# Involution weights loaded behind the first expert layer and prepared in the second norm

## The chip, the cores and the metric

One Trainium2 chip, one core of it. The time is the device time of one execution in microseconds (us), the median of several runs. TensorE multiplies matrices, VectorE and ScalarE work on elements, GpSimd does elements and issues scattered transfers, SyncE issues the other transfers. The profile names their rows PE (PEld for its weight loads), DVE, ACT, POOL and SP; a q behind the name is the engine's instruction queue.

## The reference, cut to what matters

Four layers, each a mixer and a mixture of experts, run over x of shape (8, 32, 32, 128). Before each of the two the rows are normalised over the channels, and the result is added to x. The change touches the mixer of the second layer, an involution: each pixel has its own 3 x 3 kernel for each of 8 groups of 16 channels, computed from the pixel itself by two small matrices.

```python
def _ln_c(v, eps=1e-06):
    m = jnp.mean(v, axis=-1, keepdims=True)
    s = jnp.var(v, axis=-1, keepdims=True)
    return (v - m) / jnp.sqrt(s + eps)

def _L1_conv_ref(x, W1, b1, W2, b2):       # W1 (128, 32), W2 (32, 72)
    ...
    wgt = jnp.einsum('bhwc,cd->bhwd', x, W1) + b1
    wgt = jnp.einsum('bhwd,de->bhwe', wgt, W2) + b2
    wgt = wgt.transpose(0, 3, 1, 2).reshape(b, G, 1, kk, h, w)
    ...
    patches = jnp.stack([xp[:, i:i + h, j:j + w, :] for i in range(K) for j in range(K)], axis=3)
    ...
    out = jnp.einsum('bgokhw,bgckhw->bgchw', wgt, out)
    ...

x = x + _L0_conv_ref(_ln_c(x), ...)
t = t + _L0_ffn_ref(_ln_t(t), ...)
x = x + _L1_conv_ref(_ln_c(x), L1_conv_W1, L1_conv_b1, L1_conv_W2, L1_conv_b2)
t = t + _L1_ffn_ref(_ln_t(t), ...)
...
```

## The kernel before, in words

The kernel is a row of blocks: constants, then for each layer a norm (`norm_mixer`) and a mixer with its expert layer (`mixer_fractal`, `mixer_involution`, and so on), at the end `finish`. In a block each engine has its own list of instructions, written out by hand, and runs it in order; semaphores order the engines among each other. A block ends when all its engines are through. The residual rows stay on the chip in `k.x`, 64 tiles of 128 rows by 128 channels, 8 tiles to an image.

**The expert layers.** The router of a mixer sends each row to a place in memory that belongs to its expert (`dispatched`), and GpSimd issues these scattered writes. `Experts.sync` lets SyncE load the sorted rows back tile by tile through a ring of 16 buffers (line 993); TensorE, ScalarE, VectorE work on a tile, and GpSimd scatters the result to `returned` (line 1245). SyncE is 16 tiles ahead, so it has issued its last load well before the block ends. `Experts` takes a function `load_next`, which SyncE calls behind its last tile; the involution's expert layer already loads the weights of the third layer's mixer that way (`SplineWeights.load`), the first expert layer loads nothing.

**The norm blocks.** SyncE loads the returned rows of the eight images, one transfer each (line 277). With two choices per row GpSimd adds the two (line 285); the first layer has one choice, and GpSimd has nothing to do in the second norm. VectorE adds each image to the residual (line 302) and takes statistics of its 8 tiles (line 304). After the last image it finishes the statistics (lines 240 to 246), ScalarE takes the root (line 349), and VectorE and ScalarE normalise the tiles between them (lines 321 and 356). TensorE turns each image to channel-major order (line 341) and ScalarE copies it into `channel_major` with its border (line 364). The third norm already has a preparation in front of the image loop: `spline.prepare` on VectorE, `spline.turn` on TensorE.

**The involution's block.** It opens with a preparation. SyncE loads ten small pieces: W2 and b1 four times each, for four groups of 32 partitions (lines 1710 and 1711), W1 and b2 (lines 1712 and 1713), and waits for them; then come the bias columns, the gate (lines 506 and 507) and the expert weights (line 513). GpSimd makes the gather matrices with a memset and two selects (lines 1726 to 1731). VectorE, once the ten loads are there, copies W1 four times side by side (line 1828), splits W2 in three bf16 parts (lines 1831 to 1835), places these (line 1839) and spreads them over the channels with 24 copies (line 1843), the last 8 of them for the row of the bias. TensorE then turns the bias row into 9 columns (line 1740) and VectorE copies these to `b2` (line 1848). Behind that the first product of the block runs (line 1751, `hidden(0, 0)`), which needs W1 and the image alone; ScalarE and VectorE split its result in bf16 parts (lines 1797 to 1803, 1857 to 1865), and the loop over 8 images of 2 x 9 taps begins: TensorE computes the kernel entries (lines 1761 and 1762), VectorE multiplies them with the shifted image (line 1877), TensorE adds up (line 1770). The router of an image runs between the taps of the next image.

Of the kernel before, what the change touches and what calls it, by code (L numbers as in the profile page):

```python
# [245 lines left out]
    ch.link(dve.scalar_tensor_tensor(out=var4, in0=spare, scalar=4.0 / C, in1=var4, op0=ALU.mult, op1=ALU.add))  # L246


def norm_mixer(k, layer, spline=None):

    nc = k.nc
    choices = FFN[layer - 1]["K"] if layer else 0
# [12 lines left out]
    with ExitStack() as ctx, nc.Block() as block:  # L265
        if choices:
# [1003 lines left out]
        sp.dma_start(dst[:, j:j + 1], v.rearrange("(c a) -> c a", a=1)).then_inc(sem.h, 16)  # L1270


def mixer_fractal(k):

# [21 lines left out]
    with ExitStack() as ctx, nc.Block() as block:  # L1296
# [345 lines left out]
    route.done()  # L1642


def mixer_involution(k, load_next):

# [2 lines left out]


    nc, i = k.nc, k.ins
    RED = i["L1_conv_W1"].shape[1]
    TAPS = 9
    GROUPS = i["L1_conv_W2"].shape[1] // TAPS
    GC = C // GROUPS
    PER = 2 * TAPS
    names = ("inv_loaded", "inv_prep", "inv_bias", "inv_ones", "inv_hidden", "inv_part", "inv_rest", "inv_kernel", "inv_product",
             "inv_sum", "inv_stored")  # L1660
    s = {n: k.sem(n) for n in names}
    loads = 16 * (4 * 2 + 2)
    PREP = 1 + 5 + 8 + 3 + 1

    def when(name, n):
        return s[name].h, s[name].base + n
# [2 lines left out]
    with ExitStack() as ctx, nc.Block() as block:  # L1669
# [12 lines left out]
        used = 2 * FFN[1]["E"] * FFN[1]["F"]  # L1682
        spans = k.wts[:, used:used + TAPS * C].bitcast(BF16).rearrange("p (x n) -> p x n", x=2)
        span_a, span_b = spans[:, 0], spans[:, 1]
        gather = k.wts[:, used + TAPS * C:used + 2 * TAPS * C].rearrange("p (t c) -> p t c", t=TAPS)
        left = used + 2 * TAPS * C
# [3 lines left out]
        bias_row = k.flat(k.rows1)[0:1, 0:TAPS * C]  # L1690

        def mixed(b):

# [4 lines left out]
        w1 = sb("reduce_w", [P, RED])  # L1698
        w1r = sb("reduce_w_four_times", [P, 4, RED])
        w2 = sb("span_w", [P, GROUPS * TAPS])  # L1700
        w2p = sb("span_w_parts", [P, 5, GROUPS * TAPS], BF16)
        b2row = sb("span_b_row", [1, GROUPS * TAPS])
        b1 = sb("reduce_b", [P, 1])
        b2 = sb("span_b", [P, TAPS])

        @block.sync
        def _(sp):
            for g in range(4):
                rows = slice(RED * g, RED * (g + 1))
                sp.dma_start(w2[rows, :], i["L1_conv_W2"]).then_inc(s["inv_loaded"].h, 16)  # L1710
                sp.dma_start(b1[rows, :], i["L1_conv_b1"].rearrange("(c a) -> c a", a=1)).then_inc(s["inv_loaded"].h, 16)
            sp.dma_start(w1[:], i["L1_conv_W1"]).then_inc(s["inv_loaded"].h, 16)
            sp.dma_start(b2row[:], i["L1_conv_b2"].rearrange("(a c) -> a c", a=1)).then_inc(s["inv_loaded"].h, 16)
# [8 lines left out]

        @block.gpsimd
        def _(pool):

            pool.memset(gather, 1.0).then_inc(s["inv_ones"].h, 1)
            pool.wait_ge(*when("inv_ones", 1))
            pool.affine_select(out=gather, in_=gather, compare_op=ALU.is_ge, fill=0.0, base=0,
                               pattern=[[P, TAPS], [-TAPS, C]], channel_multiplier=1).then_inc(s["inv_ones"].h, 1)
            pool.wait_ge(*when("inv_ones", 2))  # L1730
            pool.affine_select(out=gather, in_=gather, compare_op=ALU.is_ge, fill=0.0, base=TAPS - 1,
                               pattern=[[-P, TAPS], [TAPS, C]], channel_multiplier=-1).then_inc(s["inv_ones"].h, 1)
            route.send_most(pool)
            ex.gpsimd(pool)

        @block.tensor
        def _(pe):
            pe.wait_ge(*when("inv_prep", PREP - 1))
            for tap in range(TAPS):
                ins = pe.matmul(k.ps[:, 0, tap:tap + 1], bias_row[:, tap * P:(tap + 1) * P], k.ident[0:1, 0:1],  # L1740
                                start=True, stop=True)
            ins.then_inc(s["inv_bias"].h, 1)
# [44 lines left out]

        @block.scalar
        def _(act):
            act.wait_ge(*when("inv_loaded", loads))  # L1790
# [33 lines left out]

        @block.vector
        def _(dve):
            dve.wait_ge(*when("inv_loaded", loads))
            dve.tensor_copy(w1r[:], w1[:].unsqueeze(1).to_broadcast([P, 4, RED])).then_inc(s["inv_prep"].h, 1)

            ch = Chain(dve, s["inv_prep"], s["inv_prep"].base + 1)  # L1830
            ch.link(dve.tensor_copy(w2p[:, 0, :], w2[:]))
            ch.link(dve.tensor_tensor(w2[:], w2[:], w2p[:, 0, :], ALU.subtract))
            ch.link(dve.tensor_copy(w2p[:, 1, :], w2[:]))
            ch.link(dve.tensor_tensor(w2[:], w2[:], w2p[:, 1, :], ALU.subtract))
            ch.link(dve.tensor_copy(w2p[:, 2, :], w2[:]))
            for x, parts in ((3, (0, 1, 0, 1)), (4, (2, 0, 2, 1))):
                for g, part in enumerate(parts):
                    rows = slice(RED * g, RED * (g + 1))
                    ch.note(dve.tensor_copy(w2p[rows, x, :], w2p[rows, part, :]))
            ch.settle()  # L1840
            for p, dst, src in ((P, span_a, w2p[:, 3, :]), (P, span_b, w2p[:, 4, :]), (1, bias_row, b2row[:])):
                for g in range(GROUPS):
                    ins = dve.tensor_copy(
                        dst[:, g * GC * TAPS:(g + 1) * GC * TAPS].rearrange("p (c t) -> p c t", t=TAPS),
                        src[:, g * TAPS:(g + 1) * TAPS].unsqueeze(1).to_broadcast([p, GC, TAPS]))
                ins.then_inc(s["inv_prep"].h, 1)
            dve.wait_ge(*when("inv_bias", 1))
            dve.tensor_copy(b2[:], k.ps[:, 0, 0:TAPS]).then_inc(s["inv_prep"].h, 1)
            dve.wait_ge(*when("inv_prep", PREP))

            def leave(b, half):

                h = 2 * b + half
# [489 lines left out]
def build(nc, ins, out):  # L2343
    with ExitStack() as ctx:
        k = Core(nc, ctx, ins, out)
        constants(k)
        norm_mixer(k, 0)
        mixer_fractal(k)
        norm_mixer(k, 1)
        with ExitStack() as spline_ctx:  # L2350
            weights = SplineWeights(k, spline_ctx)
            mixer_involution(k, weights.load)
            norm_mixer(k, 2, weights)
            mixer_spline(k, weights)
        norm_mixer(k, 3)
# [31 lines left out]
```

## Time and profile before

| what | us |
|---|---|
| median of 3 runs | 2304.84 (2304.82 to 2305.32) |
| profiled execution: its span, first to last instruction | 2301.3 |
| second norm's block, first transfer to the next block's first | 557.43 to 602.91 |
| involution's block, opening to its first product (line 1751) | 602.91 to 618.92 |
| TensorE busy over the span | 1745.5 (76%) |
| VectorE busy over the span | 1545.8 (67%) |
| mean granted clock of TensorE, of full speed | 0.880 |

The profiled execution has no other time than its span. A timeline row reads: start, duration, engine, line, operation, what it writes <- what it reads, shape, count, and in brackets how long the engine stood idle before it and what released it. Rows of several instructions give the time from the first to the last. In the rows of stretches each engine's busy time is followed by its count of instructions, and at the end stand the granted clock (1.00 is 2.4 GHz, 0.50 is 1.2 GHz), the share of the DMA engines and GB/s.

### The profile page before, as it was taken

The numbers are of one execution on the slowest core, as the hardware profiler recorded it, in microseconds if no ns is written. First come the engines' busy times: TensorE is split into PE (matmuls) and PEld (weight loads), VectorE is DVE, ScalarE is ACT, GpSimd is POOL, SyncE is SP. The second block draws the span as 40 slices with busy tenths as digits, with TensorE's granted clock in tenths as the row PEclk, the third lists the DMA queues.
The fourth block names the chain that finished last, engine by engine and source line by source line (L and its number), as shares of the span: only waits on it lengthen the run. The fifth ranks groups of instructions, "written<-read, shape, count | busy, mean of one in ns | idle before, by whom it ended". The sixth has DMA issues, their size and how long they took to land. (4 is left out here: it accounts for less than half of the span.)

```text
span 2301.3 us, 46320 instructions
## 1 busy us (share of the span) xinstructions
PE 1745.5 (76%) x10964; PEld 1375.2 (60%) x10981; DVE 1545.8 (67%) x4675; ACT 1183.7 (51%) x2659; POOL 981.1 (43%) x969
## 2 busy tenths in 40 slices
PE   1488666994488888999981776879639999888992
PEld 1133666994244343899981344767627777687992
DVE  6898887776677777654448676646486777754554
ACT  2445776894323333776663333556535444455661
POOL 0000134552004343664444177777630355466662
PEclk9799767997699999999995787789869999989996
DMA  3001102223201011232224112233332011123326
GB/s 75 1 1 37 47 28 59 69 75 89 75 3 35 24 33 54 66 97 67 60 57 145 45 53 78 71 99 101 99 137 88 22 36 38 50 72 98 92 76 223
DMA packets 183551, 153.81 MB, mean 67 GB/s; under 512 B 40290, under 2 KB 162818, under 8 KB 183358
## 3 DMA queue, kind: packets, MB, share of 16 engines
q1 hardware_dynamic: 153406, 92.37, 14.8%
q0 software_dynamic: 29952, 59.26, 7.6%
q8 instruction: 74, 1.21, 0.2%
q14 instruction: 119, 0.97, 0.1%
HBM read 85.33 MB, written 68.79 MB: 67 GB/s over the span
## 5 line engine op out<-in xcount | busy, mean ns | idle before, releaser
L1245 POOL DMA_INDIRECT returned<-rows_second_choice x488 | 482.3, 988 | 306.9 <-DVE rows_second_choice L1175 114.3
L1042 PE MATMUL psum<-rows_first_choice 128*128 128x128 f32 x3360 | 470.7, 281 | 7.8 <-DVE rows_first_choice L1156 7.8
L1052 PE MATMUL psum<-expert_weights,rows_first_choice 128*128 x2784 | 425.6, 289 | 57.6 <-ACT rows_first_choice L1109 18.4
L1042 PEld LDWEIGHTS psum<-rows_first_choice 128*128 128x128 f32 x3360 | 428.9, 198 | 9.8 <-DVE rows_first_choice L1156 9.6
L1052 PEld LDWEIGHTS psum<-expert_weights,rows_first_choice 128*128 128x128 f32 x2784 | 360.1, 196 | 95.4 <-issue 89.4
L1109 ACT ACTIVATE rows_first_choice<-psum,bias_columns 128x128 f32<-128x128 f32 x1104 | 323.5, 368 | 162.9 <-PE psum L1042 148.8
L820 POOL DMA_INDIRECT dispatched<-rows_first_choice,slot x192 | 194.9, 1015 | 492.4 <-DVE rows_second_choice L720 439.4
L820 POOL DMA_INDIRECT dispatched<-rows_second_choice,slot x192 | 187.7, 978 | 58.5 <-issue 58.2
L1150 DVE COPY rows_first_choice<-expert_weights 128x512 f32 (+1 forms) x272 | 107.1, 394 | 144.0 <-PE psum L1042 118.9
L341 PE MATMUL psum<-identity,rows_first_choice 128*128 128x128 f32 x256 | 45.9, 341 | 193.1 <-DVE rows_first_choice L321 143.4
L1175 DVE SCALAR_TENSOR_TENSOR rows_second_choice<-psum,rows_second_choice,rows_first_choice 128x128 f32<-128x128 f32 x344 | 119.3, 347 | 98.8 <-PE psum L1052 96.3
L820 POOL DMA_INDIRECT dispatched<-rows_first_choice,expert_weights x64 | 62.0, 968 | 266.8 <-DVE rows_first_choice L718 249.4
L1092 ACT ACTIVATE rows_first_choice<-expert_weights 128x512 f32 x216 | 136.8, 634 | 49.0 <-issue 48.8
L341 PEld LDWEIGHTS psum<-identity,rows_first_choice 128*128 128x128 f32 x256 | 38.1, 179 | 200.2 <-DVE rows_first_choice L321 180.0
L1156 DVE COPY rows_first_choice<-psum 128x128 f32<-128x128 f32 x488 | 137.4, 282 | 10.9 <-PE psum L1034 10.2
L1034 PE MATMUL psum<-identity,rows_second_choice 128*128 128x128 f32 x488 | 137.1, 282 | 6.4 <-DMA rows_second_choice<-dispatched 6.4
L1112 ACT ACTIVATE rows_first_choice<-rows_first_choice,rows_second_choice 128x128 f32 x344 | 141.2, 410 | 0.0
L1162 DVE TENSOR_TENSOR rows_first_choice<-rows_first_choice,psum 128x256 f32<-128x256 f32 x144 | 60.6, 421 | 111.9 <-ACT rows_first_choice L1102 101.1
L2287 PE MATMUL psum<-channel_major 128*128 128x512 f32 x256 | 131.7, 598 | 1.2 <-ACT channel_major L2205 1.2
L2221 ACT ACTIVATE att_work<-psum 128x512 f32<-128x512 f32 x128 | 73.1, 596 | 89.9 <-PE psum L2287 87.6
L2296 PEld LDWEIGHTS psum<-rows_second_choice,rows_first_choice 128*128 128x128 f32 x680 | 88.7, 191 | 47.0 <-issue 34.9
L2296 PE MATMUL psum<-rows_second_choice,rows_first_choice 128*128 128x128 f32 x680 | 90.3, 276 | 5.4 <-DVE rows_first_choice L2255 5.4
(372 smaller groups left out, 3272.8 us busy)
## 6 DMA issues: line engine op xcount, KB each, us to landing
rows_second_choice<-dispatched SPq DMA_DIRECT2D x488, 65.0 KB
expert_weights<-returned SPq DMA_DIRECT2D x12, 1024.0 KB, 10.4
rows_second_choice<-returned SPq DMA_DIRECT2D x8, 1024.0 KB, 10.7
returned<-rows_second_choice POOLq DMA_INDIRECT x488
expert_weights<-in_L_ffn_w SPq DMA_DIRECT2D x3, 2048.0 KB, 8.3
residual<-in_x SPq DMA_DIRECT2D x8, 512.0 KB, 7.2
rows_first_choice<-returned SPq DMA_DIRECT2D x4, 1024.0 KB, 8.8
out<-residual SPq DMA_DIRECT2D x8, 512.0 KB, 6.0
```

Source lines behind the costliest of these rows:

```text
L820: pool.indirect_dma_start(out=self.k.dispatched, out_offset=bass.IndirectOffsetOnAxis(ap=self.slot[:, b % 2, c, t:t + 1], axis=0), in_=sel ...
L1034: pe.transpose(k.ps[:, self.PSX + u % 2, 0:P], self.rt[:, u, 0:C], k.ident[:]).then_inc(self.s["x_turned"].h, 1)
L1042: ins = pe.matmul(k.ps[:, self.PSH + u % 2, j * P:(j + 1) * P], self.wc[:, u % 2, j * P:(j + 1) * P], self.xt[:, u % 2, :], start=True, st ...
L1052: ins = pe.matmul(self.result_bank(u), self.gs[:, u % self.HB, j * P:(j + 1) * P], self.second[:, bass.ds(e, 1), j, :].rearrange("p a c -> ...
L1092: act.activation(self.wc[:, u % 2, :], self.first[:, bass.ds(e, 1), :].rearrange("p a f -> p (a f)"), ACT.Copy).then_inc(self.s["w_copied" ...
L1109: ins = act.activation(self.hs[:, u % self.HB, cols], k.ps[:, self.PSH + u % 2, cols], f["act"], bias=self.bcol[:, bass.ds(e * self.J + j, ...
L1112: act.activation(self.wb[:, u % 4, :], self.b2rows[:, bass.ds(e, 1), :].rearrange("p a c -> p (a c)"), ACT.Copy, scale=self.rt[:, u, C + 1 ...
L1156: dve.tensor_copy(self.xt[:, u % 2, :], k.ps[:, self.PSX + u % 2, 0:P]).then_inc(self.s["x_copied"].h, 1)
L1175: ins = dve.scalar_tensor_tensor(out=self.ys[:, u, :], in0=self.result_bank(u), scalar=weight, in1=self.wb[:, u % 4, :], op0=ALU.mult, op1 ...
L1245: pool.indirect_dma_start(out=k.returned[0:N * self.K, :], out_offset=bass.IndirectOffsetOnAxis(ap=self.rt[:, u, C:C + 1].bitcast(I32), ax ...
L2287: pe.matmul(k.ps[:, g % 4, :], xft[:, b * IMG + j * P:b * IMG + (j + 1) * P], xft[:, b * IMG + h * BANK:b * IMG + (h + 1) * BANK], start=T ...
L2296: ins = pe.matmul(k.ps[:, 4 + h, t * P:(t + 1) * P], r2[g % 3][:, t * P:(t + 1) * P], val[:, b, j * P:(j + 1) * P], start=(j == 0 and t == ...
```

## The change

A class `InvolutionWeights` now holds the involution's weights and the code that prepares them. The ten loads are given to the first expert layer as its `load_next`, so that SyncE issues them behind the last tile of rows and waits for them there. In the second norm GpSimd makes the gather matrices, VectorE runs the preparation before the image loop (with the bias row spread first and the two spans behind it), TensorE turns the bias row before its transposes, into PSUM bank 4, and VectorE copies the 9 columns behind the statistics of the last image. The involution's block begins with its first product. Most of the preparation's buffers move from tiles of their own into parts of larger tiles that are free at that time.

```diff
-def norm_mixer(k, layer, spline=None):
+def norm_mixer(k, layer, spline=None, involution=None):
...
+        if involution:
+            @block.gpsimd
+            def _(pool):
+                involution.make_gather(pool)
+
...
             if spline:
                 spline.prepare(dve)
+            if involution:
+                involution.prepare(dve)
             for b in range(B):
...
                 for t in range(b * TPB, (b + 1) * TPB):
                     ch.note(dve.bn_stats(k.stats[:, t, :], k.x[:, t, :]))
+            if involution:
+                involution.take_bias(dve)
             ch = Chain(dve, s["norm_step"], s["norm_step"].base + B * per)
             ch.settle()
             finish_stats(dve, k, ch)
...
             if spline:
                 spline.turn(pe)
+            if involution:
+                involution.turn(pe)
...
-        ex = Experts(k, 0, ctx, route)
+        ex = Experts(k, 0, ctx, route, load_next)
...
+class InvolutionWeights:
...
+        spare, temporary, last = k.flat(k.rows0)[:, N:], k.flat(k.rows1)[:, 2 * IMG:], k.wts[:, 12288 - 2 * P:]
...
+    def load(self, sp):
+        i, RED, sem = self.k.ins, self.RED, self.s["inv_loaded"]
+        for g in range(4):
+            rows = slice(RED * g, RED * (g + 1))
+            sp.dma_start(self.w2[rows, :], i["L1_conv_W2"]).then_inc(sem.h, 16)
+            sp.dma_start(self.b1[rows, :], i["L1_conv_b1"].rearrange("(c a) -> c a", a=1)).then_inc(sem.h, 16)
+        sp.dma_start(self.w1[:], i["L1_conv_W1"]).then_inc(sem.h, 16)
+        sp.dma_start(self.b2row[:], i["L1_conv_b2"].rearrange("(a c) -> a c", a=1)).then_inc(sem.h, 16)
+        sp.wait_ge(*self.when("inv_loaded", self.loads))
+
+    def prepare(self, dve):
...
+        dve.wait_ge(*self.when("inv_loaded", self.loads))
+        dve.tensor_copy(self.w1r[:], self.w1[:].unsqueeze(1).to_broadcast([P, 4, RED])).then_inc(s["inv_prep"].h, 1)
...
+        for p, dst, src in ((1, self.bias_row, self.b2row[:]), (P, self.span_a, w2p[:, 3, :]), (P, self.span_b, w2p[:, 4, :])):
...
+    def take_bias(self, dve):
+        dve.wait_ge(*self.when("inv_bias", 1))
+        dve.tensor_copy(self.b2[:], self.k.ps[:, self.BANK, 0:self.TAPS]).then_inc(self.s["inv_prep"].h, 1)
+
+    def turn(self, pe):
+        pe.wait_ge(*self.when("inv_prep", self.PREP - 3))
+        for tap in range(self.TAPS):
+            ins = pe.matmul(self.k.ps[:, self.BANK, tap:tap + 1], self.bias_row[:, tap * P:(tap + 1) * P],
+                            self.k.ident[0:1, 0:1], start=True, stop=True)
+        ins.then_inc(self.s["inv_bias"].h, 1)
+
+    def make_gather(self, pool):
+        s, gather, TAPS = self.s, self.gather, self.TAPS
+        pool.memset(gather, 1.0).then_inc(s["inv_ones"].h, 1)
...
-def mixer_involution(k, load_next):
+def mixer_involution(k, weights, load_next):
...
         @block.sync
         def _(sp):
-            for g in range(4):
...
-            sp.wait_ge(*when("inv_loaded", loads))
             ex.sync_early(sp)
...
         def _(pe):
-            pe.wait_ge(*when("inv_prep", PREP - 1))
...
-            pe.wait_ge(*when("inv_ones", 3))
-            pe.wait_ge(*when("inv_prep", PREP))
-
...
-        mixer_fractal(k)
-        norm_mixer(k, 1)
+        involution = InvolutionWeights(k, ctx)
+        mixer_fractal(k, involution.load)
+        norm_mixer(k, 1, involution=involution)
...
-            mixer_involution(k, weights.load)
+            mixer_involution(k, involution, weights.load)
```

## Rows read from the trace of the kernel before

**Rows 1.** The page's chain that ended last, by engine.
```profile
SPq 1%; DMA 0%; DVE 0%; issue 0%; DVEq 0%
```

**Rows 2.** Busy time, involution opening: us, PE, PEld, DVE, ACT, POOL, clock, DMA, GB/s.
```profile
602.91:618.92 16.01, 3.99 (x19) 3.94 (x19) 5.76 (x39) 0.00 (x0) 3.48 (x3) 0.52 0.40 66
```

**Rows 3.** Timeline of the opening of the involution's block.
```profile
601.61 1.03 ACT L364 ACTIVATE channel_major<-psum 128x1024 f32<-128x1024 f32 x1 [0.28 <-PE psum L341]
602.91 1.06 POOL L1726 MEMSET expert_weights<- 128x1152 f32 x1 [54.22 <-POOLq L265]
602.91 0.36 SPq L1710 DMA_DIRECT2D span_w<-in_L_conv_W  x1
...
605.33 1.21 POOL L1731 TENSOR_SCALAR_AFFINE_SELECT expert_weights<-expert_weights 128x1152 f32<-128x1152 f32 x1
...
608.51 0.23 DVE L1828 COPY reduce_w_four_times<-reduce_w 128x128 f32<-128x128 f32 x1 [9.83 <-DMA span_b_row<-in_L_conv_b]
...
613.30 1.21 DVE L1843 COPY rows_second_choice<-span_b_row 1x144 f32<-1x144 f32 x8
614.21 1.46 SPq L513 DMA_DIRECT2D expert_weights<-in_L_ffn_W  x2
...
614.57 3.99 PE L1740 MATMUL psum<-identity,rows_second_choice 1*128 1x1 f32 x18 [13.00 <-DVE rows_second_choice L1843]
618.60 0.17 DVE L1848 COPY span_b<-psum 128x9 f32<-128x9 f32 x1 [4.08 <-PE psum L1740]
...
618.92 2.05 PE L1751 MATMUL psum<-channel_major,reduce_w_four_times 128*128 128x512 f32 x2 [0.35 <-DVE span_b L1848]
...
626.34 0.63 PE L1762 MATMUL psum<-rows_first_choice,expert_weights 128*128 128x512 bf16 x1 [5.37 <-DVE rows_first_choice L1865]
```

**Rows 4.** Timeline of the second norm's block.
```profile
557.43 6.82 SPq L277 DMA_DIRECT2D expert_weights<-returned  x6
...
561.28 1.23 DVE L302 TENSOR_TENSOR residual<-residual,expert_weights 128x1024 f32<-128x1024 f32 x1 [15.14 <-DMA expert_weights<-returned]
...
583.82 0.27 DVE L240 TENSOR_TENSOR mean<-bn_stats 128x64 f32<-128x64 f32 x1
```

**Rows 5.** Stretches around the opening, and the whole tap loop.
```profile
603.00:603.50 0.50, 0.00 (x0) 0.00 (x0) 0.00 (x0) 0.00 (x0) 0.50 (x1) 0.91 0.00 0
603.50:604.00 0.50, 0.00 (x0) 0.00 (x0) 0.00 (x0) 0.00 (x0) 0.47 (x1) 0.50 0.06 9
621.00:626.00 5.00, 0.00 (x0) 0.07 (x2) 2.17 (x5) 3.08 (x5) 0.00 (x0) 0.50 1.04 391
630.50:631.00 0.50, 0.50 (x3) 0.37 (x2) 0.00 (x0) 0.50 (x1) 0.00 (x0) 0.78 0.00 0
626.30:921.70 295.40, 249.63 (x913) 118.85 (x927) 218.27 (x604) 93.13 (x142) 101.54 (x104) 0.95 0.10 30
```

**Rows 6.** Timeline of TensorE, a later product of the same kind.
```profile
640.77 1.02 PE L1751 MATMUL psum<-channel_major,reduce_w_four_times 128*128 128x512 f32 x2
```

**Rows 7.** Timeline of the third norm's opening, GpSimd beside VectorE.
```profile
1206.72 11.43 SPq L277 DMA_DIRECT2D expert_weights<-returned  x6
...
1206.80 0.29 DVE L1944 MEMSET hats_at_zero<- 128x1 f32 x9 [5.32 <-PEq L1669]
...
1216.34 17.77 POOL L285 TENSOR_TENSOR expert_weights<-expert_weights 128x1024 f32<-128x1024 f32 x6 [13.60 <-issue]
...
1218.70 3.35 DVE L302 TENSOR_TENSOR residual<-residual,expert_weights 128x1024 f32<-128x1024 f32 x1 [4.46 <-POOL expert_weights L285]
...
1223.65 1.69 DVE L302 TENSOR_TENSOR residual<-residual,expert_weights 128x1024 f32<-128x1024 f32 x1
```

**Rows 8.** What SyncE's queue waited for: total, times, longest, in us.
```profile
SPq L1296 <- PEq L1296: 36.8, 1, 36.8
```

**Rows 9.** Timeline of TensorE, the first products of the gate.
```profile
670.82 1.85 PE L559 MATMUL psum<-gate_w,turned_rows 128*128 128x8 f32 x16
```

**Rows 10.** Line 1857: minimum, median, maximum in ns; first and last start.
```profile
L1857 DVE SCALAR_TENSOR_TENSOR hidden_rest<-psum,reduce_b,rows_first_choice x16: 742/751/752, 621.9 to 891.3; 128x512 f32<-128x512 f32 x16
```

More of the change, by code:

```diff
@@ L1270, in load_columns, with mixer_fractal @@
         sp.dma_start(dst[:, j:j + 1], v.rearrange("(c a) -> c a", a=1)).then_inc(sem.h, 16)
-def mixer_fractal(k):
+def mixer_fractal(k, load_next):
     nc, i = k.nc, k.ins
@@ L1642, in mixer_fractal, with __init__, sb, when @@
     route.done()
-def mixer_involution(k, load_next):
+class InvolutionWeights:
+    TAPS = 9
+    BANK = 4
+    PREP = 1 + 5 + 8 + 3 + 1
+    def __init__(self, k, ctx):
+        nc, i = k.nc, k.ins
+        self.k = k
+        self.RED = RED = i["L1_conv_W1"].shape[1]
+        self.GROUPS = i["L1_conv_W2"].shape[1] // self.TAPS
+        self.GC = C // self.GROUPS
+        self.loads = 16 * (4 * 2 + 2)
+        def sb(name, shape, dt=F32):
+            return ctx.enter_context(nc.sbuf_tensor(name, shape, dt))
+        TAPS, GROUPS = self.TAPS, self.GROUPS
+        self.used = used = 2 * FFN[1]["E"] * FFN[1]["F"]
+        spans = k.wts[:, used:used + TAPS * C].bitcast(BF16).rearrange("p (x n) -> p x n", x=2)
+        self.span_a, self.span_b = spans[:, 0], spans[:, 1]
+        self.gather = k.wts[:, used + TAPS * C:used + 2 * TAPS * C].rearrange("p (t c) -> p t c", t=TAPS)
+        spare, temporary, last = k.flat(k.rows0)[:, N:], k.flat(k.rows1)[:, 2 * IMG:], k.wts[:, 12288 - 2 * P:]
+        wide = GROUPS * TAPS
+        self.w1, self.w2 = spare[:, 0:RED], spare[:, RED:RED + wide]
+        self.w1r = last[:, 0:4 * RED].rearrange("p (a r) -> p a r", a=4)
+        self.b2row = last[0:1, P:P + wide]
+        self.bias_row = temporary[0:1, 0:TAPS * C]
+        self.w2p = temporary[:, TAPS * C:TAPS * C + 5 * wide // 2].bitcast(BF16).rearrange("p (x n) -> p x n", x=5)
+        self.b1 = sb("reduce_b", [P, 1])
+        self.b2 = sb("span_b", [P, TAPS])
+        self.s = {n: k.sem(n) for n in ("inv_loaded", "inv_prep", "inv_bias", "inv_ones")}
+    def when(self, name, n):
+        return self.s[name].h, self.s[name].base + n
+    def load(self, sp):
[8 more added lines that the diff above has]
+    def prepare(self, dve):
+        s, w2, w2p, RED, TAPS, GROUPS, GC = self.s, self.w2, self.w2p, self.RED, self.TAPS, self.GROUPS, self.GC
+        dve.wait_ge(*self.when("inv_loaded", self.loads))
+        dve.tensor_copy(self.w1r[:], self.w1[:].unsqueeze(1).to_broadcast([P, 4, RED])).then_inc(s["inv_prep"].h, 1)
+        ch = Chain(dve, s["inv_prep"], s["inv_prep"].base + 1)
+        ch.link(dve.tensor_copy(w2p[:, 0, :], w2[:]))
+        ch.link(dve.tensor_tensor(w2[:], w2[:], w2p[:, 0, :], ALU.subtract))
+        ch.link(dve.tensor_copy(w2p[:, 1, :], w2[:]))
+        ch.link(dve.tensor_tensor(w2[:], w2[:], w2p[:, 1, :], ALU.subtract))
+        ch.link(dve.tensor_copy(w2p[:, 2, :], w2[:]))
+        for x, parts in ((3, (0, 1, 0, 1)), (4, (2, 0, 2, 1))):
+            for g, part in enumerate(parts):
+                rows = slice(RED * g, RED * (g + 1))
+                ch.note(dve.tensor_copy(w2p[rows, x, :], w2p[rows, part, :]))
+        ch.settle()
+        for p, dst, src in ((1, self.bias_row, self.b2row[:]), (P, self.span_a, w2p[:, 3, :]), (P, self.span_b, w2p[:, 4, :])):
+            for g in range(GROUPS):
+                ins = dve.tensor_copy(
+                    dst[:, g * GC * TAPS:(g + 1) * GC * TAPS].rearrange("p (c t) -> p c t", t=TAPS),
+                    src[:, g * TAPS:(g + 1) * TAPS].unsqueeze(1).to_broadcast([p, GC, TAPS]))
+            ins.then_inc(s["inv_prep"].h, 1)
+    def take_bias(self, dve):
[10 more added lines that the diff above has]
+        pool.memset(gather, 1.0).then_inc(s["inv_ones"].h, 1)
+        pool.wait_ge(*self.when("inv_ones", 1))
+        pool.affine_select(out=gather, in_=gather, compare_op=ALU.is_ge, fill=0.0, base=0,
+                           pattern=[[P, TAPS], [-TAPS, C]], channel_multiplier=1).then_inc(s["inv_ones"].h, 1)
+        pool.wait_ge(*self.when("inv_ones", 2))
+        pool.affine_select(out=gather, in_=gather, compare_op=ALU.is_ge, fill=0.0, base=TAPS - 1,
+                           pattern=[[-P, TAPS], [TAPS, C]], channel_multiplier=-1).then_inc(s["inv_ones"].h, 1)
@@ L1653, in mixer_involution @@
+def mixer_involution(k, weights, load_next):
     nc, i = k.nc, k.ins
[L1654 to L1657, printed above, removed]
+    RED, TAPS, GROUPS, GC = weights.RED, weights.TAPS, weights.GROUPS, weights.GC
+    w1r, b1, b2, span_a, span_b, gather = (weights.w1r, weights.b1, weights.b2, weights.span_a, weights.span_b,
+                                           weights.gather)
     PER = 2 * TAPS
-    names = ("inv_loaded", "inv_prep", "inv_bias", "inv_ones", "inv_hidden", "inv_part", "inv_rest", "inv_kernel", "inv_product",
-             "inv_sum", "inv_stored")
+    names = ("inv_hidden", "inv_part", "inv_rest", "inv_kernel", "inv_product", "inv_sum", "inv_stored")
@@ L1661, in mixer_involution @@
     s = {n: k.sem(n) for n in names}
-    loads = 16 * (4 * 2 + 2)
-    PREP = 1 + 5 + 8 + 3 + 1
     def when(name, n):
@@ L1681, in mixer_involution @@
         prods = [k.flat(k.rows1)[:, tail][:, 0:BANK], k.flat(k.rows1)[:, tail][:, BANK:2 * BANK]]
[L1682 to L1686, printed above, removed]
+        left = weights.used + 2 * TAPS * C
         mixed_first = k.wts[:, left:left + IMG]
@@ L1697, in mixer_involution @@
         ex = Experts(k, 1, ctx, route, load_next)
[L1698 to L1704, printed above, removed]
         @block.sync
         def _(sp):
-            for g in range(4):
[L1709 to L1713, printed above, removed]
-            sp.wait_ge(*when("inv_loaded", loads))
             ex.sync_early(sp)
@@ L1724, in _ @@
         def _(pool):
[L1726 to L1732, printed above, removed]
             route.send_most(pool)
@@ L1737, in _ @@
         def _(pe):
-            pe.wait_ge(*when("inv_prep", PREP - 1))
[L1739 to L1742, printed above, removed]
-            pe.wait_ge(*when("inv_ones", 3))
-            pe.wait_ge(*when("inv_prep", PREP))
             LAG = 3
@@ L1789, in _ @@
         def _(act):
-            act.wait_ge(*when("inv_loaded", loads))
             def bias(b, half):
@@ L1826, in _ @@
         def _(dve):
[L1827 to L1849, printed above, removed]
             def leave(b, half):
```

1 line of the change is left out of this document (removed).

## The prediction

> **What bounds the kernel now.** I read the page's chain of waits first: it holds only the last 1.2% of the span, the output stage [rows 1]. The kernel is a row of blocks, and an engine enters the next block only when all have left the last, so the stage's own views decide. The busy times of the opening of the involution's block come second [rows 2]: in its first 16.01 us TensorE is busy 3.99 us, ScalarE not at all, VectorE 5.76 us. The reader is to see a block in which nothing but preparation runs. The timeline says in which order [rows 3]. SyncE issues ten small loads from 602.91 on; VectorE starts at 608.51, released by the last of them after 9.83 us idle; its preparation ends at 613.30 + 1.21 = 614.51; TensorE's bias products run from 614.57 to 618.56; VectorE copies them (0.17 us); the first useful product of the block (L1751) starts at 618.92. GpSimd's three operations (602.91 to 605.33 + 1.21 = 606.54) wait for nobody and nobody waits for them last. Then the timeline of the norm block before it, where the work goes [rows 4]: SyncE enters at 557.43, VectorE waits until 561.28 for the first returned rows and from there works without a gap until 583.82. The norm block is bound by VectorE, with 3.8 us of slack at its opening and none behind.
>
> **The change part by part.** All terms are differences in one profiled execution of 2301.3 us; its only time shown is that span, and the timed runs are 3.5 us longer, which I take as fixed.
>
> *The opening goes.* TensorE's first product needs only the channel-major image and the prepared weights, both there when the block opens. GpSimd and SyncE issue at 602.91; I put TensorE 0.04 us behind, at 602.95: 618.92 - 602.95 = 15.97 us less. The next thing late is the chain behind that product (ScalarE's split and VectorE's rest, up to TensorE's 626.34), which moves along unchanged.
>
> *The first product is quicker.* Today it runs with TensorE long cold: 2.05 us for the pair [rows 3]. The granted clock is still high after the norm's last transposes: 0.91 of full speed averaged over 603.0 to 603.5, and 0.50, the 1.2 GHz level, only from 603.5 on [rows 5]. A product that starts at 602.95 meets the 2.4 GHz level, at which the same pair takes 1.02 us later in the loop [rows 6]: 1.03 us less, bounds 0 and 1.03. TensorE then idles about 5.37 us as today [rows 3]. The level fell at 603.5, some 1.9 us after the last transposes, which ScalarE's last copy (601.61) had waited for; so it should be low again when the taps come, as it is now: from 626.34 until about 630.6, where the clock is 0.78 in a half microsecond [rows 5]. If the high level should last, these 4.3 us of work would take half, 2.1 us less. I take nothing for it.
>
> *VectorE's preparation enters the norm.* The same 38 instructions, 608.51 to 614.51, are 6.00 us, in another order (bias row first) at the same cost. In the third norm block, which already opens with such a preparation, VectorE starts 0.08 us behind SyncE [rows 7]; so here at 557.51, and it ends at 563.51 instead of being ready for the rows at 561.28: 2.23 us more, all of it on the path, since VectorE has no gap behind. 3.77 of the 6.00 us lie in the old wait. Were that cover gone, the price would be 6.0.
>
> *GpSimd now works beside VectorE.* Its three operations take 3.63 us alone and start together with the preparation. Before, they had VectorE to themselves, so the trace has no row of this pair. The nearest rows are in the third norm, where GpSimd adds while VectorE adds: the same 128x1024 addition took 1.23 us with GpSimd idle [rows 4], 1.69 beside it, and 3.35 once, at the start of the overlap [rows 7]. From below: 0, the preparation's copies being short and of one input, save two. From above: VectorE stands still for all of it, 3.63 us. I take the steady row, as a share: 3.63 x (1 - 1.23/1.69) = 1.0 us more.
> The Trainium skill speaks against this part: "SBUF — State Buffer", section "SBUF: two separate sides", says that the port pair which VectorE and GpSimd share is locked by whichever instruction comes first for its whole length, while the other waits. The row of 3.35 us looks like such a lock, the 1.69 us rows do not stand still so long.
>
> *The copy of the bias.* One VectorE copy of 0.17 us stands between the statistics and their finish: 0.17 more, bounds 0 and 0.3. Behind its wait are queued VectorE's finish of the statistics and, through it, ScalarE's root. The wait itself costs nothing: the bias products start when 22 of the 38 instructions are done, last 3.99 us [rows 3], and so end near 567, while the statistics run to 583.82 today. TensorE's transposes, queued behind those products, are not due before the statistics either.
>
> *The ten loads move* to SyncE's queue behind the last rows of the first expert layer. They take 608.51 - 602.91 = 5.6 us with their landing. SyncE today waits 36.8 us at the end of that block [rows 8], so they are hidden six times over; uncovered they would cost those 5.6 us. Nothing is queued behind them. In the involution's block SyncE goes straight to the bias columns, the gate and the expert weights. The gate's loads are over when the weights are issued, at 614.21 today [rows 3]; after the change that is 614.21 - 608.51 = 5.7 us into the block. Their first user is TensorE at 670.82 [rows 9], 67.9 us into the block today and 51 after the change. The weights now land while the first taps run instead of before them. VectorE's 16 instructions of line 1857, the first of which ran while the DMA engines moved 391 GB/s [rows 5], took 742 to 752 ns each [rows 10], so I charge nothing.
>
> *Sum:* -15.97 - 1.03 + 2.23 + 1.0 + 0.17 = -13.6 us. The span becomes 2287.7 and the median 2304.84 - 13.6 = 2291.2 us, 0.59% less. Every later block starts when the involution ends, so the gain should last to the end.
>
> **The rivals.**
> *Full lock:* VectorE gets nothing done during GpSimd's 3.63 us. Instead of 1.0 the term is 3.63: -11.0, 2293.9 us. For it, the 3.35 us row; against it, the 1.69 us rows, and that the preparation is mostly tiny copies. By the skill's rule of the lock, named above, this is the case that should come, at least for the two additions and whichever copies use both ports.
> *Clock kept:* the high level lasts until the taps: 2.1 us less again, 2289.1 us. For it, that TensorE comes to this gap at the high level, not the low one; against it, that it lasted some 1.9 us in the gap of today, and the gap before the taps is 5.4 us.
> *Gain hidden:* the loop's start, or the first router, turns out to be held by something that the preparation covered, such as the weights now landing amid the taps, or the loads are not hidden. Then the wait only changes its name: about 2303 us. Against it stand rows 8 to 10.
> *Slower:* TensorE's clock in the tap loop. The loop is TensorE's (busy 249.63 of 295.40 us) and its granted clock averages 0.95 [rows 5], that is 10% of it, 29.5 us, at the lower level. A loop that starts in another state could fall more often at the gaps between images. Each us at the low level does half its work, so it costs 0.5 us. The 13.6 us are eaten from 27.2 more such us on (19% of the loop), and it is slower by 0.2% from 36.4 on (22%). At 25% the time is 2304.84 - 13.6 + 22.2 = 2313.4 us. Against it: the falls come where the router's work opens gaps in TensorE, which does not change.
>
> **How the numbers follow.** Forecast 0.64, full lock 0.14, clock kept 0.10, gain hidden 0.07, slower 0.05. The likeliest case by itself reaches from 2289.1 to 2293.9. For the range I add the loss of the quick first product (1.0), the smallest contention (-1.0) and the clock's changes further on, of about 2 us: 2289.1 - 3.0 = 2286.1 to 2293.9 + 3.0 = 2296.9. About 0.2%, 4.6 us, is what a measurement of this kernel tells from no change. Faster by more: the first three cases and part of the fourth, 0.91; within: 0.05; slower: 0.04.
>
> **What would show it.** The norm block's first residual addition (L302) should start near 564.5 instead of 561.28, the block should end some 3.4 us later, near 606, and the first L1751 pair should follow the last norm copy within 0.5 us and take about 1 us. GpSimd's memset and two selects should lie beside VectorE's copies; if these stretch from 6 to over 9 us, the lock is right. The loads should be done near 526, far ahead of the block's end at 557. The interval from the first L1751 to the first expert tile should keep its length; if it grows by several us, look at the clock. The prediction is wrong if the first L1751 is released by a wait for anything but the block's opening, or if the tap loop grows by more than the opening saves.

## The result and the profile after

The changed kernel takes 2278.30 us (median of 4 runs, 2276.42 to 2279.92) against 2304.83 (4 runs, 2304.63 to 2305.32): ratio 0.9882 [0.9869, 0.9896], 26.5 us less. The forecast of 2291.2 us has the right sign and half the size; 2278.30 lies below its range.

The span is 2274.7 us, 26.6 less than before, and the mean granted clock 0.883 (before 0.880). I read the timeline at five places, in order of time. The first is the opening of the second norm, to be read beside [rows 4] and the preparation of [rows 3].

```profile
557.65 1.06 POOL L1742 MEMSET expert_weights<- 128x1152 f32 x1 [8.73 <-POOLq L1307]
557.65 6.90 SPq L277 DMA_DIRECT2D expert_weights<-returned  x6
557.68 1.10 DVE L1709 COPY expert_weights<-rows_first_choice 128x128 f32<-128x128 f32 x1 [11.31 <-PEq L1307]
557.83 0.99 DVE L1712 CAST rows_second_choice<-rows_first_choice 128x72 bf16<-128x72 f32 x1
558.78 1.22 POOL L1744 TENSOR_SCALAR_AFFINE_SELECT expert_weights<-expert_weights 128x1152 f32<-128x1152 f32 x1
558.86 1.22 DVE L1713 TENSOR_TENSOR rows_first_choice<-rows_first_choice,rows_second_choice 128x72 f32<-128x72 f32 x1
560.06 1.21 POOL L1747 TENSOR_SCALAR_AFFINE_SELECT expert_weights<-expert_weights 128x1152 f32<-128x1152 f32 x1
560.11 1.21 DVE L1714 CAST rows_second_choice<-rows_first_choice 128x72 bf16<-128x72 f32 x1
561.35 0.23 DVE L1715 TENSOR_TENSOR rows_first_choice<-rows_first_choice,rows_second_choice 128x72 f32<-128x72 f32 x1
...
564.66 1.85 DVE L1724 COPY expert_weights<-rows_second_choice 128x144 bf16<-128x144 bf16 x16
...
566.43 1.20 DVE L309 TENSOR_TENSOR residual<-residual,expert_weights 128x1024 f32<-128x1024 f32 x1
...
588.83 0.15 DVE L1731 COPY span_b<-psum 128x9 f32<-128x9 f32 x1
588.94 0.27 DVE L240 TENSOR_TENSOR mean<-bn_stats 128x64 f32<-128x64 f32 x1
```

The block opens at 557.65. Four of VectorE's small operations take 0.99 to 1.22 us, and each ends within 0.11 us behind GpSimd's operation beside it (GpSimd's end at 558.71, 560.00 and 561.27); once GpSimd is through, the same kind takes 0.23. The preparation lasts from 557.68 to 566.51, 8.83 us instead of 6.00. The first residual addition starts 8.78 us after the opening (before: 3.85).

The second and third places are the opening of the involution's block and the end of its tap loop, beside [rows 3].

```profile
607.78 0.37 SPq L993 DMA_DIRECT2D bias_columns<-in_L_ffn_b  x1
...
607.82 1.10 PE L1818 MATMUL psum<-channel_major,expert_weights 128*128 128x512 f32 x2 [1.37 <-PEq L265]
...
613.75 0.61 PE L1828 MATMUL psum<-rows_first_choice,expert_weights 128*128 128x512 bf16 x1 [4.83 <-DVE rows_first_choice L1906]
...
900.58 0.42 DVE L1161 COPY rows_first_choice<-expert_weights 128x512 f32 x1
```

```profile
913.21 0.41 DVE L1150 COPY rows_first_choice<-expert_weights 128x512 f32 x1
```

The first product comes 0.04 us behind the opening, released by it, and is a quick one. The taps start at 613.75, 12.59 us earlier than 626.34. At the expert layer's first copy of weights (the row behind is the kernel before's) 12.63 us are gained: the tap loop is what it was.

The fourth place is the opening of the third norm, before at 1206.72 [rows 7]:

```profile
1181.28 1.02 SPq L277 DMA_DIRECT2D expert_weights<-returned  x2
```

The gain is 25.44 us here, so another 12.8 us came in the second expert layer, which the change doesn't touch. From here to the end of the span it grows by 1.2 more. The fifth place is therefore the loop of that layer. First ScalarE's timeline in the kernel before, then what it waited for at this line (total, times, longest, in us), before and after.

```profile
1079.33 1.14 ACT L1109 ACTIVATE rows_first_choice<-psum,bias_columns 128x128 f32<-128x128 f32 x4 [0.46 <-PE psum L1042]
1080.34 0.42 ACT L1112 ACTIVATE rows_first_choice<-rows_first_choice,rows_second_choice 128x128 f32 x1
1086.14 1.14 ACT L1109 ACTIVATE rows_first_choice<-psum,bias_columns 128x128 f32<-128x128 f32 x4 [5.38 <-issue]
...
1122.73 1.14 ACT L1109 ACTIVATE rows_first_choice<-psum,bias_columns 128x128 f32<-128x128 f32 x4 [5.40 <-issue]
```

```profile
ACT rows_first_choice L1109 <- issue: 11.8, 7, 5.4
```

```profile
ACT rows_first_choice L1120 <- issue: 3.5, 12, 0.5
```

Twice ScalarE stood still for 5.4 us and waited for nothing that the profile shows, 36.6 us apart: where its loop over 16 tiles jumps back. After the change no such wait is over 0.5 us. What TensorE lost by it is in the stretches, before and after (us, PE, PEld, DVE, ACT, POOL, clock, DMA, GB/s):

```profile
1080.00:1090.00 10.00, 5.65 (x43) 5.42 (x42) 2.69 (x9) 3.53 (x13) 2.27 (x3) 0.91 0.18 50
1090.00:1100.00 10.00, 10.00 (x85) 10.00 (x85) 4.79 (x15) 6.90 (x25) 4.91 (x5) 0.92 0.16 46
1117.00:1127.00 10.00, 5.63 (x38) 5.40 (x38) 2.26 (x7) 3.10 (x12) 2.10 (x3) 0.76 0.18 50
```

```profile
1067.00:1077.00 10.00, 10.00 (x92) 10.00 (x91) 5.63 (x17) 7.66 (x28) 5.62 (x6) 1.00 0.27 73
```

TensorE idles 4.35 and 4.37 us and then works at a granted clock of 0.50, the 1.2 GHz level, for about 3.4 us behind the first stall and 5.0 behind the second. At half speed these cost 1.7 and 2.5 us; with the idle time that is an estimate of 12.9 us, as much as the 12.8 gained here. After the change TensorE is busy throughout, at 1.00. The DMA queues of the stretch 1080.5 to 1086.5 before, and of 1067 to 1073 after (the same jump back), say what happened (packets, MB, share of 16 engines):

```profile
q1 hardware_dynamic: 525, 0.25, 18.5%
q0 software_dynamic: 96, 0.20, 9.2%
q14 instruction: 4, 0.03, 1.7%
```

```profile
q1 hardware_dynamic: 576, 0.27, 19.5%
q0 software_dynamic: 97, 0.20, 9.8%
```

The stalled stretch holds four fetches of instructions, of 8 KB each, the other none. The same queue over the whole span, from the pages of before and after:

```profile
q14 instruction: 119, 0.97, 0.1%
```

```profile
q14 instruction: 109, 0.89, 0.1%
```

Of the twelve profiles behind this document the three with stalls show 119 such packets, the other nine 109 or 110. In ScalarE's program the change makes one difference ahead of this loop: the wait for the ten loads (`inv_loaded`) is gone, one instruction, and everything behind it stands one place earlier.

### The profile page after: what moved, and what is told of

Its sections match the earlier page's. It is cut to its first block and busy times, and to the rows that moved or that the text cites. A ratio compares the mean times of both kernels' runs of the same rounds, so it can differ in the third digit from the quotient of the medians.

```text
span 2274.7 us, 46334 instructions
## 1 busy us (share of the span) xinstructions
PE 1743.1 (77%) x10980; PEld 1372.8 (60%) x10981; DVE 1546.3 (68%) x4675; ACT 1182.3 (52%) x2659; POOL 978.9 (43%) x969
## 5 line engine op out<-in xcount | busy, mean ns | idle before, releaser
L1063 PE MATMUL psum<-expert_weights,rows_first_choice 128*128 x2784 | 423.1, 288 | 47.7 <-issue 13.5
## 6 DMA issues: line engine op xcount, KB each, us to landing
expert_weights<-returned SPq DMA_DIRECT2D x12, 1024.0 KB, 10.3
```

The source lines that it names most:

```text
L1063: ins = pe.matmul(self.result_bank(u), self.gs[:, u % self.HB, j * P:(j + 1) * P], self.second[:, bass.ds(e, 1), j, :].rearrange("p a c -> ...
```

## The experiments

My theory A: half of the gain has nothing to do with the preparation; it is the place of ScalarE's loop in its program. Its rival: the changed weights, or the earlier start, make the second expert layer run better. For the norm block: GpSimd's operations hold VectorE's small ones for their whole length (the lock), or only slow them.

**Only the wait removed** (the kernel before, without it)

```diff
-            act.wait_ge(*when("inv_loaded", loads))
```

> The kernel before, with one thing out: ScalarE's own wait for the ten loads at the head of the involution's block. It is covered by the wait behind it, so no work moves. Theory A (ScalarE's program: two stalls of 5.4 us of ScalarE in the second expert layer, at 1080.7 and 1117.3, come from how its loop lies in the program; one instruction less shifts it): the stalls go, and with them what the clock loses behind them, about 13 us in all, so about 2292 us, ratio near 0.994. Theory B (the stalls come from when the loop runs, beside which transfers; the changed kernel runs it 12.6 us earlier): nothing changes, 2304.8 us within 1.

2290.6 us, ratio 0.9937 [0.9921, 0.9954]. The third norm opens 12.9 us earlier (timeline), 11.8 of it gained behind the first tap, which starts 1.1 earlier; and the stalls are gone (waits of ScalarE's line):

```profile
ACT rows_first_choice L1109 <- issue: 3.7, 12, 0.5
```

```profile
1193.83 1.13 SPq L277 DMA_DIRECT2D expert_weights<-returned  x2
```

One instruction that never made ScalarE late is worth 13.5 us by the medians (2304.14 in these runs).

**The change with the wait put back**

```diff
+            act.wait_ge(*weights.when("inv_loaded", weights.loads))
```

> The changed kernel with the same wait of ScalarE put back at the head of the involution's block, where it is long fulfilled. Theory A: the two stalls of about 5.4 us come back in the second expert layer, and the time is about 2278.3 + 13 = 2291 us, ratio near 0.994, which is what the prediction's terms gave. Theory B: no stalls, 2278 us, ratio near 0.988.

2293.87 us, ratio 0.9953 [0.9936, 0.9969]: the change at the old place of the loop gains 10.3 us, which lies within the forecast's range. The stalls are back, both of them, and the third norm opens 15.6 us later than in the changed kernel; why the same two stalls cost more here than before the change is open.

```profile
1075.41 1.14 ACT L1120 ACTIVATE rows_first_choice<-psum,bias_columns 128x128 f32<-128x128 f32 x4 [5.62 <-issue]
...
1112.66 1.14 ACT L1120 ACTIVATE rows_first_choice<-psum,bias_columns 128x128 f32<-128x128 f32 x4 [5.53 <-issue]
...
1196.87 2.45 SPq L277 DMA_DIRECT2D expert_weights<-returned  x3
```

**GpSimd's three operations later** (the changed kernel; they wait for the norm's sixth image, away from the preparation)

```diff
+                pool.wait_ge(*when("norm_most", B - 2))
                 involution.make_gather(pool)
```

> The changed kernel with GpSimd's gather matrices made later: GpSimd waits for the sixth image's normalised tiles, when VectorE has a few us to spare, instead of starting beside VectorE's preparation. Theory lock (VectorE's first copies of 0.2 us took 1.0 to 1.2 us each because GpSimd's memset and selects held them): the preparation takes 6.0 us again instead of 8.8, the first residual addition starts 2.8 us earlier, and the time falls by 2.8 to about 2275.5 us. Rival (VectorE was slow at the block's opening for another reason, its code or the landing transfers): the copies stay at 1.0 to 1.2 us and the time stays at 2278 us.

2278.01 us, ratio 0.9878 [0.9861, 0.9895], no gain. But the preparation is back at 6.0 us, and the first addition comes 5.99 us after the opening instead of 8.78. Part of what was won is lost at the block's other end, where GpSimd now meets the normalisation:

```profile
559.10 0.23 DVE L1710 COPY expert_weights<-rows_first_choice 128x128 f32<-128x128 f32 x1 [11.32 <-PEq L1308]
559.24 0.19 DVE L1713 CAST rows_second_choice<-rows_first_choice 128x72 bf16<-128x72 f32 x1
...
565.05 1.20 DVE L310 TENSOR_TENSOR residual<-residual,expert_weights 128x1024 f32<-128x1024 f32 x1
...
601.83 1.21 POOL L1748 TENSOR_SCALAR_AFFINE_SELECT expert_weights<-expert_weights 128x1152 f32<-128x1152 f32 x1
603.68 1.09 PE L353 MATMUL psum<-identity,rows_first_choice 128*128 128x128 f32 x8 [1.96 <-DVE rows_first_choice L331]
```

The 48 normalisations of VectorE take 15.1 us in the block, 12.4 in the changed kernel; TensorE waits for them. The block takes 48.58 us, 1.55 less than the changed kernel's 50.13, but in this profile it opened 1.4 us later. TensorE's granted clock is 0.91 there from 420 to 440, in the first expert layer, where it is 1.00 in the changed kernel: about 1.7 us of TensorE's work, an estimate. What lowered it is open.

**The preparation out of the norm as well** (behind VectorE's last tile of the first expert layer; GpSimd as in the last one)

```diff
+            prepare_next(dve)          # in mixer_fractal, behind ex.vector(dve)
...
-            if involution:             # in norm_mixer
-                involution.prepare(dve)
```

> As the last one, and VectorE's 38 instructions of preparation moved once more, to the end of the first expert layer's block, where VectorE stands idle for 11 us (its temporaries lie 2176 columns further on, clear of the ring of rows). If the whole delay of the second norm's first residual addition is the preparation in front of it, that addition starts 3.8 us after the block opens, as before the change, instead of 8.8 us, and the time is about 2278.3 - 4.9 = 2273.4 us. Rival (the delay is partly the returned rows landing later): less than 2.8 us of it comes back, 2275.5 us or more.

2278.12 us, ratio 0.9881 [0.9865, 0.9898]. The preparation ran where VectorE was idle, from 548.04 to 554.37, and the first addition now waits for its rows (4.29 us after the opening). GpSimd again stretched the normalisation to 15.1 us. The block took 47.79 us (559.43 to 607.22) after 50.13 in the changed kernel, but opened 1.8 us later, behind the same 0.91 from 420 to 440, and the time did not move. These two runs left the place for GpSimd open: the norm block's opening, where VectorE now waits anyway.

**Preparation in the expert layer, GpSimd at the norm's opening**: the last kernel without the wait for `norm_most`, and with it, in the same runs, **the changed kernel once more**.

> The changed kernel with VectorE's preparation behind its last tile of the first expert layer (as in the run before it with that move) and GpSimd's three gather operations at the opening of the norm block, where VectorE now only waits for the first returned rows. No operation of GpSimd then lies beside one of VectorE. Lock theory: the first addition of the norm block starts about 4.3 us after the block's opening instead of 8.8, no normalisation is stretched at the end, the involution's block opens 4.5 us earlier against the norm block's opening, about 2274 us. Rival (the norm block is held by something else by then, the first returned rows or TensorE): as the two runs before, about 2278 us.

> The changed kernel itself, for its spread and as the mark for the three beside it: 2276 to 2280 us, no stall of ScalarE in the second expert layer.

2272.38 us (2271.75 to 2274.60), ratio 0.9866 [0.9850, 0.9882], against 2277.78 (2277.06 to 2279.50), ratio 0.9889 [0.9872, 0.9905]. The intervals overlap a little, but all runs of this version lie below all of the changed kernel's. Its norm block, in the timeline:

```profile
556.81 1.06 POOL L1741 MEMSET expert_weights<- 128x1152 f32 x1 [8.73 <-POOLq L1305]
556.82 7.14 SPq L277 DMA_DIRECT2D expert_weights<-returned  x6
...
559.23 1.21 POOL L1746 TENSOR_SCALAR_AFFINE_SELECT expert_weights<-expert_weights 128x1152 f32<-128x1152 f32 x1
561.32 1.22 DVE L307 TENSOR_TENSOR residual<-residual,expert_weights 128x1024 f32<-128x1024 f32 x1 [9.56 <-DMA expert_weights<-returned]
...
603.05 1.52 PE L1817 MATMUL psum<-channel_major,expert_weights 128*128 128x512 f32 x2 [1.38 <-PEq L265]
```

The block takes 46.2 us (50.1 in the changed kernel), 3.9 less where 4.5 was expected, and the normalisation is back at 12.4. The other 1.5 us between the medians are not located. So GpSimd delays VectorE's copies and its normalisations, and here its place was free where VectorE had nothing to do.

Not everything of VectorE is held. In the kernel before, GpSimd's additions of the third norm [rows 7] lie beside the statistics of most images, and those take as long as they do alone, at the end:

```profile
1225.37 1.64 DVE L304 BATCH_NORM_STATS2 bn_stats<-residual 128x6 f32<-128x128 f32 x8
...
1244.60 1.65 DVE L304 BATCH_NORM_STATS2 bn_stats<-residual 128x6 f32<-128x128 f32 x8
```

Beside the second norm's own 64 such instructions GpSimd's three operations were not tried.

**Where the loop stalls: two, three, four and five places on.** The changed kernel with the wait written 3, 5, 7 or 9 times; two such waits are put into one instruction, so these count 2, 3, 4 and 5 (ScalarE's rows in the trace: 7396, 7397, 7398 and 7399, against 7394 in the changed kernel and 7395 with one wait).

```diff
+            for _ in range(3):         # 5, 7, 9
+                act.wait_ge(*weights.when("inv_loaded", weights.loads))
```

> The changed kernel with ScalarE's wait for the ten loads written three times at the head of its list in the involution's block. Two of the three become instructions of their own, so ScalarE's loops of the second expert layer stand two instructions further on than in the changed kernel, one further than in the kernel before. Counted in ScalarE's program the second loop (258 instructions) begins at 2376 in the changed kernel (no stall), at 2377 in the kernel before (two stalls of 5.4 us) and at 2378 here. Theory A (a single bad place: the loop is just longer than one block of fetched instructions, and only where its first instruction is the last of a block does it touch a third): the stalls are gone again, third norm near 1181, about 2278 us. Rival B (from a certain place on the loop no longer fits): both stalls stay, third norm near 1197, about 2294 us.

> The changed kernel with the same wait written nine times, which puts ScalarE's two loops of the second expert layer five instructions further on: the first loop from 2116 to 2121, the second from 2376 to 2381. The bad place of theory A, 2377, repeats every 256 instructions, so 2121 is one too. Theory A: no stall at the second loop, but two of about 5.4 us at the first loop's two jumps back, near 977 and 1007 us, so again about 2294 us. Rival B (from a certain place on): the two stalls stay at the second loop, near 1070 and 1107. Rival C (the stalls hang on the time at which the loop is entered, not on its place): none or others, about 2278 us.

> The same with the wait written five times: loops three instructions further on (second loop from 2379). Theory A with 259: no stall, about 2278 us. Rival (bad places in no order that the count explains): stalls, at the first loop or the second, about 2294 us.

> The changed kernel with ScalarE's wait written seven times: loops four instructions further on than in the changed kernel (second loop from 2380 by the program's count). At five places on theory A, in the form that the bad place repeats every 256 instructions, failed: no stall at the first loop. In the trace 259 instructions, not 260, lie from one loop's jump back to the next loop's (the jump between the loops, which only falls through, leaves no record). If that jump is not there, the first loop's bad place is one earlier. Theory A with 259: two stalls of about 5.4 us at the first loop, near 977 and 1007 us, about 2294 us. If there is no stall, the repeat is not shown, and the one bad place stands alone.

| places on | us | stalls of 5 us and more |
|---|---|---|
| 0 (changed kernel) | 2277.78 | none |
| 1 (wait put back) | 2293.87 | two, second loop |
| 2 | 2278.14, ratio 0.9887 [0.9871, 0.9904] | none |
| 3 | 2275.33, one run | none |
| 4 | 2294.01, one run | two, first loop |
| 5 | 2277.69, ratio 0.9884 [0.9868, 0.9901] | none |

Two places on, the stalls are gone: there is no threshold (rival B falls), and of the six places tried one is bad for the second loop, as theory A says. Five places on I had expected them at the first loop and was wrong by one: I had counted 260 instructions from loop to loop; the records hold 259 in order of issue (by start times some of the traces show 260). That the one too many was a jump that only falls through is not shown. Four places on they came at the first loop, near the time expected:

```profile
982.58 1.14 ACT L1120 ACTIVATE rows_first_choice<-psum,bias_columns 128x128 f32<-128x128 f32 x4 [5.89 <-issue]
...
1020.64 1.14 ACT L1120 ACTIVATE rows_first_choice<-psum,bias_columns 128x128 f32<-128x128 f32 x4 [5.57 <-issue]
```

In the kernel before the second loop stood badly. Here everything stands three places further on than there, and the first loop, 259 ahead of the second, stands badly: the two bad places are 256 apart. The loop has 258 instructions; ScalarE's loops of 194 and 147 in the later layers jump back without such a stall in all twelve profiles. Both would follow from fetches in blocks of 256 instructions: the loop then touches three blocks only where its first instruction is the last of one. That is worked out from where it stalls; the records show the four packets in a stall, not which instructions they hold. The Trainium skill, "Runtime: NRT & Kernel Launch", section "Instruction fetch mechanics", says that the instruction memory of most engines holds two blocks of 256 and that a taken branch out of that window must wait for a fetch; the runs agree with it, and their price is the 5.4 to 5.9 us above. From the first tap to the opening of the third norm the three profiles with stalls take 580.4 to 583.7 us, the nine without 566.6 to 568.6.

## Why the prediction was wrong

Up to the first taps its steps came as forecast, with one term too small; it was wrong on what follows them.

| step | predicted us | measured us |
|---|---|---|
| first product, from the block's opening | -15.97 | -15.97 (16.01 to 0.04) |
| first product quicker | -1.03 | -0.95 (2.05 to 1.10) |
| the chain behind it, up to the first tap | 0 | -0.54 (5.37 to 4.83 of waiting) |
| VectorE's preparation and GpSimd beside it | +2.23 + 1.0 | +4.93 (3.85 to 8.78) |
| bias copy, rest of the norm block | +0.17 | -0.28 (41.63 to 41.35) |
| norm block opens | 0 | +0.22 |
| **to the first tap** | **-13.6** | **-12.6** |
| from there to the third norm | 0 | -12.85 |
| third norm to the end | 0 | -1.16 |

*The failed step* is the last sentence of the sum: "Every later block starts when the involution ends, so the gain should last to the end", that is, no term for the blocks behind. The missing term is -12.85 us: ScalarE's two stalls, together 10.8 us, in which TensorE idles 8.7, and TensorE's lower clock behind them. Taking away the wait alone gave it (-12.9 at the third norm), putting it back took it away (+15.6), and other places of the loop did the same with no wait that was ever late. Both stalls stood in the trace of before as the longest waits of ScalarE on "issue". The prediction goes through the change part by part, but the wait that is taken from ScalarE is not among the parts. That its sign came out right is the preparation's doing; the second half of the gain was luck.

*The mis-sized term* is the contention: +1.0 predicted, and the preparation became 2.83 us longer. I had taken the steady additions of [rows 7] as the nearest row and short copies of one input as the lower end; the copy and the casts were held as long as the subtraction of two inputs. The full lock, priced at 3.63, was the better case: from the first operation to the fifth it is 3.67 us, where it is 0.87 with GpSimd moved away, so 2.80 are lost. The Trainium skill's "SBUF — State Buffer", section "SBUF: two separate sides", has the rule that whichever of the two first takes the ports that they share shuts the other out for its whole instruction. Here the trace agrees: VectorE's four operations end within 0.11 us behind GpSimd's. By the terms up to the first tap the gain was 12.6; by the medians it is 10.3 with the stalls on both sides and 12.3 without them on either (2290.60 to 2278.30). All lie near the forecast's 13.6.

*Right*: the loads were hidden (issued from 520.71 to 525.91; SyncE still waited 30.1 us at the end of that block), the weights landing amid the first taps cost nothing, the tap loop kept its length (286.83 us against 286.87), and the first product found the high clock: 1.00 from 607.78 to 609.00, where the same pair had 0.50 before. The level was low again when the taps began, as forecast (0.50 from 613.75 to 615). The high clock is not sure in every execution: the pair took 1.52 us at 0.67 with the preparation in the expert layer and GpSimd at the norm's opening, and 1.97 at 0.53 with the loop two places on.

*Open*: the 0.28 us in the norm block, and, but for the two profiles with a clock of 0.91, why the norm block opens between 556.2 and 557.7. The second profile of the changed kernel shows how far one goes: 13.7 us to the first tap, 12.3 from there to the third norm, and 0.1 lost behind it, with 0.14 in place of the 0.54 of the chain. So terms of up to about 1 us in the table, the 1.16 among them, are within what two profiles of one kernel differ by. The runs of the kernel before spread over 0.7 us beside the changed kernel, but from 2302.08 to 2309.24 beside the first experiments; the changed kernel's spread over 3.5 and 2.4. The cause is open.

## What to carry to other kernels

When a change adds or removes even one instruction ahead of a hardware loop, look in the profile of before for "issue" stalls at that loop's jumps back, and count them as a term that may appear or vanish: here 13 us for one wait. The loops here that stalled have 258 instructions; other lengths above 256 were not run. Before crediting such a gain to the change, put the removed instruction back alone. And GpSimd's work is not free beside VectorE's copies, casts and normalisations: here 3.5 us of it cost 2.7 to 2.8. It was free where VectorE was idle, and the statistics were not stretched by it.

## What the runs showed of the hardware

- A jump back of ScalarE's loop of 258 instructions costs 5.4 to 5.9 us at two places 256 instructions apart (the second loop's one place on, the first loop's four places on) and under 0.6 at the others tried, from 0 to 5 places on; four or five instruction packets of 8 KB lie in the stretch of a stall, and a kernel with two stalls has 9 or 10 more of them.
- Beside GpSimd's memset and selects of 1.06 to 1.22 us, VectorE's copies of 0.19 to 0.23 us took 0.99 to 1.22, the one beside the memset too. Its 48 normalisations, in SBUF, lost 2.7 us to 3.5 us of GpSimd's work. Eight bn_stats took 1.64 us beside GpSimd's additions and 1.65 alone.
